# Routed gate and up projections with the weights stationary and the tokens streaming, each tile's weights brought from DRAM into a ring of six

## What is computed

```python
logits = jnp.einsum('th,eh->te', xt.astype(jnp.float32), w_router.astype(jnp.float32))
scores = jax.nn.sigmoid(logits)
topk_w, topk_i = jax.lax.top_k(scores, TOPK)
topk_w = topk_w / jnp.sum(topk_w, axis=-1, keepdims=True)
...
gate = jax.nn.silu(jnp.einsum('th,eih->tei', xt, wg))
up = jnp.einsum('th,eih->tei', xt, wu)
expert_out = jnp.einsum('tei,ehi->teh', gate * up, wd)
out = jnp.einsum('te,teh->th', comb, expert_out)
sgate = jax.nn.silu(jnp.einsum('th,jih->tji', xt, sg))
sup = jnp.einsum('th,jih->tji', xt, su)
out = out + jnp.einsum('tji,jhi->th', sgate * sup, sd)
```

## Time and profile before

| | |
|---|---|
| median of 3 runs | 445.16 us (443.85 to 445.98) |
| the profiled execution: its time | 445.5 us |
| the profiled execution: its span | 443.7 us |
| TensorE matmul busy | 395.6 us, 89% |
| TensorE loads busy | 289.1 us, 65% |
| DVE, ACT, POOL busy | 257.2, 205.5, 90.5 us |
| DMA traffic | 42.48 MB; HBM read 24.81 MB, written 17.31 MB |

### The profile page before, as it was taken

The page is one execution under the profiler, slowest core; times in us unless marked ns, Lnnn a source line. Parts: engine busy times, 40 slices in busy tenths (PEclk is TensorE's granted clock), DMA queues, the critical chain, the costliest instruction groups (busy, mean ns, idle before and its releaser), DMA issues.

```text
span 443.7 us, 7225 instructions
## 1 busy us (share of the span) xinstructions
PE 395.6 (89%) x2295; PEld 289.1 (65%) x2296; DVE 257.2 (58%) x814; ACT 205.5 (46%) x519; POOL 90.5 (20%) x100
## 2 busy tenths in 40 slices
PE   3877787787988999997999999999999999999991
PEld 2445464555765878776888886666667676766660
DVE  3799999899887784785474424343333333433330
ACT  4597999999854668420120213232232323232320
POOL 6656140001000022121312000212121212121221
PEclk9998999999998999998999999999999999999997
DMA  6199999100000001000698300122212222221212
GB/s 172 27 353 343 339 354 429 60 1 1 1 1 1 2 7 67 1 24 27 242 429 347 88 2 24 26 36 38 36 38 39 35 46 33 39 36 24 24 12 24
DMA packets 22988, 42.48 MB, mean 96 GB/s; under 512 B 1968, under 2 KB 20976, under 8 KB 21680
## 3 DMA queue, kind: packets, MB, share of 16 engines
q1 hardware_dynamic: 17632, 35.76, 23.3%
q0 software_dynamic: 4080, 5.18, 7.4%
q10 hardware_dynamic: 1248, 1.18, 0.8%
HBM read 24.81 MB, written 17.31 MB: 95 GB/s over the span
## 4 chain that ended last, share of the span: by engine, by line
PE 59%; DVE 19%; ACT 14%; POOL 3%; issue 2%; DMA 2%; POOLq 0%; DVEq 0%
PE ps_z L749 13%; PE ps_o L775 11%; PE ps_gu L749 9%; ACT weights L843 6%; PE ps_pt L605 5%; PE ps_z L598 5%; DVE weights L1041 5%; PE ps_gu L598 4%; DVE weights L1036 3%; ACT weights L834 3%; ACT weights L849 3%; PE ps_pt L765 3%; PE ps_gu L605 2%; DVE hidden L1094 1%; DVE gate_silu L1091 1%
## 5 line engine op out<-in xcount | busy, mean ns | idle before, releaser
L439 POOL DMA_INDIRECT out<-y_sb,tile_in x23 | 35.9, 1559 | 166.1 <-DVE y_sb L1280 163.0
L843 ACT ACTIVATE weights<-weights 128x256 f32<-128x256 f32 x128 | 64.3, 536 | 0.1
L749 PE MATMUL ps_z<-weights,tile_t 128*128 x184 | 63.2, 486 | 0.0
L775 PE MATMUL ps_o<-weights,hidden 128*128 x230 | 53.5, 380 | 0.9 <-ACT hidden L950 0.9
L1091 DVE SCALAR_TENSOR_TENSOR gate_silu<-gate_tanh,ps_z 128x256 f32<-128x256 f32 x66 | 24.5, 371 | 49.5 <-ACT gate_tanh L935 36.2
L517 PE MATMUL ps_pt<-ident,weights 128*128 128x128 f32 x256 | 35.4, 284 | 15.6 <-ACT weights L849 15.2
L749 PEld LDWEIGHTS ps_z<-weights,tile_t 128*128 128x128 f32 x184 | 33.2, 190 | 23.2 <-issue 22.0
L775 PEld LDWEIGHTS ps_o<-weights,hidden 128*128 128x128 f32 x230 | 43.6, 190 | 7.0 <-issue 1.1
L935 ACT ACTIVATE gate_tanh<-ps_gu 128x256 f32<-128x256 f32 x23 | 8.8, 383 | 80.5 <-PE ps_gu L749 80.5
L517 PEld LDWEIGHTS ps_pt<-ident,weights 128*128 128x128 f32 x256 | 29.9, 147 | 22.6 <-issue 21.8
L1036 DVE SCALAR_TENSOR_TENSOR weights<-weights 128x1024 f32<-128x1024 f32 x32 | 39.0, 1219 | 9.1 <-ACT weights L834 5.6
(11 more groups left out here) (192 smaller groups left out, 618.4 us busy)
## 6 DMA issues: line engine op xcount, KB each, us to landing
weights<-w_experts SPq DMA_DIRECT2D x8, 1920.0 KB, 14.1
slots<-pad_row SPq DMA_DIRECT2D x9, 1188.0 KB, 13.5
weights<-w_experts SPq DMA_DIRECT2D x1, 3840.0 KB, 14.5
tile_in<-slots SPq DMA_DIRECT2D x23, 132.0 KB, 2.1
out<-y_sb ACTq DMA_DIRECT2D x4, 256.0 KB, 2.2
weights<-x SPq DMA_DIRECT2D x2, 256.0 KB, 4.4
x_in<-x SPq DMA_DIRECT2D x2, 256.0 KB, 5.3
out<-y_sb,tile_in POOLq DMA_INDIRECT x23, 3.8
```

The source lines that it names most:

```text
L439: pool.indirect_dma_start(out=out, out_offset=bass.IndirectOffsetOnAxis(ap=tile_in[:, slot, ID_COL:ID_COL + 1].bitcast(U32), axis=0), in_= ...
L749: mm = pe.matmul(ps_chunk[c][:, 0:2 * cw], tile_t[:, r % 2, k, :], weights[:, bass.ds(off + (k * GU + 2 * c0), 2 * cw)], start=(k == 0), s ...
L775: mm = pe.matmul(ps_o[:, 0:D], hid_t[:, r % 2, i, :], weights[:, bass.ds(off + (KC * GU + i * D), D)], start=(i == 0), stop=(i == IC - 1))
L843: ins = act.activation(v, v, ACT.Exp, bias=neg_max[:, w % AHEAD, i:i + 1], scale=-1.0, accum_out=sums[:, L % PAIR, s:s + 1])
```

## The change

- The routed gate and up projections now have a 128x128 block of weights as stationary operand and stream the tile's 128 tokens (`gate_chunk`): 20 matmuls of 128 columns a tile in place of 4 of 512 and 2 of 256. Hidden columns come out on the partitions, and DVE writes them straight to `hid_t`.
- `turn_hidden` on TensorE, ACT's copy of its result (L950), and the semaphores between them are gone.
- In a TensorE step the down projection of tile j-1 moves ahead of chunks 1 and 2 of tile j. DVE scales tile j-1 in step j behind its first hidden chunk, one tile late where it was two.
- SBUF no longer holds the routed gate and up weights. The down weights of all eight experts (5.24 MB) are loaded in one DMA early on, behind the fill of `slots`. The gate and up weights of each tile's expert (1.31 MB: 128 partitions, 2 rows of 5,120 bytes each) are loaded for each of the 23 tiles into a ring of six places, which the attention's scratch shares; SP issues them behind the tile's rows, the first six once the table is ready, then one each time an add has landed. TensorE reads the ring at fixed addresses and waits for its semaphore at a tile's first chunk.
- The host lays the weights out in three arrays instead of one.

```diff
-        LATE = 5
-        scratch_at = [(E - LATE) * W_EXP]
+        scratch_at = [RING_AT]
...
-            for e in range(E - LATE):
-                sp.dma_start(w_exp[:, e, :], w_experts[e]).then_inc(ld_expert[e], 16)
+            sp.dma_start(weights[:, DOWN_AT:RING_AT].rearrange("p (e w) -> p e w", e=E),
+                         w_down.rearrange("e p w -> p e w")).then_inc(ld_down, 16)
+
+            def load_weights(j, place):
+                e = sp.value_load(expert_i[0:1, bass.ds(j, 1)], min_val=0, max_val=E - 1)
+                sp.dma_start(ring[place].rearrange("p (k w) -> p k w", k=KC),
+                             w_gu[bass.ds(e * (KC * P), KC * P), :].rearrange("(k p) w -> p k w", p=P)).then_inc(ld_ring[place], 16)
 
             sp.wait_ge(x_norm_ready, HV * B)
             sp.wait_ge(y_saved, PAIR)
             sp.wait_ge(st_early_rows, 16 * TOPK * HV * PAIR)
-            for e in range(E - LATE, E):
-                sp.dma_start(w_exp[:, e, :], w_experts[e]).then_inc(ld_expert[e], 16)
-
             sp.wait_ge(st_late_rows, 16 * TOPK * HV * (B - PAIR))
             sp.wait_ge(table_ready, 1)
             for j in range(SLOTS_IN):
                 load_tile(j, j)
+                load_weights(j, j)
...
                     sp.wait_ge(r_add, 16 * (j - SLOTS_IN + 1))
                     load_tile(j, s)
+                    load_weights(j, s)
...
-            def gate_chunk(q, r, c, off):
+            def gate_chunk(q, r, c):
                 j = SLOTS_IN * q + r
                 c0, cw = GATE_CHUNKS[c]
                 if c == 0:
+                    pe.wait_ge(ld_ring[r % SLOTS_IN], 16 * (q + r // SLOTS_IN + 1))
                     pe.wait_ge(r_xtc, j + 1)
                 if not isinstance(j, int) or j >= 1:
                     pe.wait_ge(r_hid, 3 * j + c - 2)
-                for k in range(KC):
-                    mm = pe.matmul(ps_chunk[c][:, 0:2 * cw], tile_t[:, r % 2, k, :],
-                                   weights[:, bass.ds(off + (k * GU + 2 * c0), 2 * cw)],
-                                   start=(k == 0), stop=(k == KC - 1))
+                for i in range(cw // P):
+                    for part, col in enumerate(gate_col(c0 // P + i)):
+                        for k in range(KC):
+                            a = k * GU + col
+                            mm = pe.matmul(ps_chunk[c][:, part * cw + i * P:part * cw + (i + 1) * P], ring[r % SLOTS_IN][:, a:a + P],
+                                           tile_t[:, r % 2, k, :], start=(k == 0), stop=(k == KC - 1))
                 mm.then_inc(r_gu, 1)
...
-            def turn_hidden(q, r):
...
-                pe.wait_ge(r_htc, j + 1)
+                pe.wait_ge(r_hid, 3 * j + 3)
...
             def step(q, r):
...
                 if inner or s >= 1:
-                    turn_hidden(q, r - 1)
-                if off is not None:
-                    gate_chunk(q, r, 1, off)
-                    gate_chunk(q, r, 2, off)
-                if inner or s >= 1:
                     down_tile(q, r - 1)
+                if inner or s < SLOT_TILES:
+                    gate_chunk(q, r, 1)
+                    gate_chunk(q, r, 2)
...
-                if inner or s >= 1:
-                    act.wait_ge(r_ht, s)
-                    act.activation(hid_t[:, (r - 1) % 2, :, :].rearrange("p a b -> p (a b)"), ps_pt[:, 0:I], ACT.Copy
-                                   ).then_inc(r_htc, 1)
...
-                if inner or s >= 2:
-                    scale_output(q, r - 2)
                 if inner or s < SLOT_TILES:
                     hidden_chunk(q, r, 0)
+                if inner or s >= 1:
+                    scale_output(q, r - 1)
+                if inner or s < SLOT_TILES:
                     hidden_chunk(q, r, 1)
                     hidden_chunk(q, r, 2)
```

More of the change, by code:

```diff
@@ L129, in build @@
         weights = sb("weights", [P, (E + NSH) * W_EXP])
+        ring = [weights[:, RING_AT + i * W_GU:RING_AT + (i + 1) * W_GU] for i in range(SLOTS_IN)]
         late_rows = [[sb(f"rows{n}{k}", [P, HV, ROW]) for k in range(TOPK)] for n in range(PAIR, B)]
@@ L219, in build @@
         ld_shared = sem("ld_shared")
-        ld_expert = [sem(f"ld_expert{e}") for e in range(E)]
+        ld_down = sem("ld_down")
+        ld_ring = [sem(f"ld_ring{i}") for i in range(SLOTS_IN)]
         const_step, ident_ready = sem("const_step"), sem("ident_ready")
@@ L747, in gate_chunk, with down_at @@
                     pe.wait_ge(r_hid, 3 * j + c - 2)
-                for k in range(KC):
-                    mm = pe.matmul(ps_chunk[c][:, 0:2 * cw], tile_t[:, r % 2, k, :],
-                                   weights[:, bass.ds(off + (k * GU + 2 * c0), 2 * cw)],
-                                   start=(k == 0), stop=(k == KC - 1))
+                for i in range(cw // P):
[4 more added lines that the diff above has]
+                                           tile_t[:, r % 2, k, :], start=(k == 0), stop=(k == KC - 1))
                 mm.then_inc(r_gu, 1)
-            def expert_at(q, r):
+            def down_at(q, r):
                 e = pe.value_load(expert_i[0:1, bass.ds(SLOTS_IN * q + r, 1)], min_val=0, max_val=E - 1)
-                return e * W_EXP
-            def turn_hidden(q, r):
[L760 to L764, removed]
-                    mm = pe.transpose(ps_pt[:, i * P:(i + 1) * P], hid[:, r % 2, i * P:(i + 1) * P], ident)
-                mm.then_inc(r_ht, 1)
+                return e * W_DOWN
             def down_tile(q, r):
                 j = SLOTS_IN * q + r
-                off = expert_at(q, r)
-                pe.wait_ge(r_htc, j + 1)
+                off = down_at(q, r)
+                pe.wait_ge(r_hid, 3 * j + 3)
                 if not isinstance(j, int) or j >= 1:
@@ L774, in down_tile @@
                 for i in range(IC):
-                    mm = pe.matmul(ps_o[:, 0:D], hid_t[:, r % 2, i, :],
-                                   weights[:, bass.ds(off + (KC * GU + i * D), D)], start=(i == 0), stop=(i == IC - 1))
+                    mm = pe.matmul(ps_o[:, 0:D], hid_t[:, r % 2, i * P:(i + 1) * P],
+                                   weights[:, bass.ds(off + (DOWN_AT + i * D), D)], start=(i == 0), stop=(i == IC - 1))
                 mm.then_inc(r_y, 1)
@@ L781, in step @@
                 inner = not isinstance(s, int)
-                off = expert_at(q, r) if inner or s < SLOT_TILES else None
-                if off is not None:
-                    gate_chunk(q, r, 0, off)
+                if inner or s < SLOT_TILES:
+                    gate_chunk(q, r, 0)
                 if inner or s + 1 < SLOT_TILES:
@@ L800, in _ @@
             shared_down(3, 1, 1)
-            for e in range(E):
-                pe.wait_ge(ld_expert[e], 16)
+            pe.wait_ge(ld_down, 16)
             step(0, 0)
@@ L1285, in step @@
                 inner = not isinstance(s, int)
-                if inner or s >= 2:
-                    scale_output(q, r - 2)
                 if inner or s < SLOT_TILES:
                     hidden_chunk(q, r, 0)
+                if inner or s >= 1:
+                    scale_output(q, r - 1)
+                if inner or s < SLOT_TILES:
                     hidden_chunk(q, r, 1)
                     hidden_chunk(q, r, 2)
-            for s in range(2):
-                step(0, s)
+            step(0, 0)
             dve.wait_ge(st_base, 16 * B)
-            for s in range(2, PEELED):
+            for s in range(1, PEELED):
                 step(0, s)
@@ L1300, in _ @@
                     step(q, r)
-            for s in range(PEELED + SLOTS_IN * ROUTED_LOOPS, SLOT_TILES + 2):
+            for s in range(PEELED + SLOTS_IN * ROUTED_LOOPS, SLOT_TILES + 1):
                 step(0, s)
@@ L1311, with gate_up_rows @@
     from concourse.bass_utils import run_bass_kernel_spmd
-    def expert_rows(gate, up, down):
+    def gate_up_rows(gate, up):
         n = gate.shape[0]
@@ L1321, in expert_rows, with down_rows, all_rows @@
             cols += [g[..., c0:c0 + cw], u[..., c0:c0 + cw]]
-        gu = np.concatenate(cols, -1).transpose(0, 2, 1, 3).reshape(n, P, KC * GU)
-        d = np.asarray(down).transpose(0, 2, 1).reshape(n, IC, P, D).transpose(0, 2, 1, 3).reshape(n, P, IC * D)
-        return np.concatenate([gu, d], -1)
+        return np.concatenate(cols, -1)
+    def down_rows(down):
+        n = down.shape[0]
+        return np.asarray(down).transpose(0, 2, 1).reshape(n, IC, P, D).transpose(0, 2, 1, 3).reshape(n, P, W_DOWN)
+    def all_rows(gate, up, down):
+        n = gate.shape[0]
+        return np.concatenate([gate_up_rows(gate, up).transpose(0, 2, 1, 3).reshape(n, P, W_GU), down_rows(down)], -1)
     arrays = {
```

36 lines of the change are left out of this document (20 added, 16 removed).

## The result

The changed kernel takes 443.03 us (median of 20 runs, 441.23 to 445.12), the kernel before beside it 445.58 us: ratio 0.9943, 95% interval 0.9926 to 0.9960. It is faster by 0.6%, where 1.9% was forecast and where the range ended at 442.5. The execution profiled took 441.58 us, one of the quicker ones; the predicted numbers are compared with it step by step.

A forecast was written before the change was run, and what follows sets the result against it. TensorE's own instructions were taken to bound the routed part. Steps -7.8, first step +0.2 and tail -1.1 gave -8.7 us from the profiled 445.5, or 436.8; less 0.3 to the median, 436.6 us, range 432.8 to 442.5.

The forecast's parts named there:

- the price of a pair: Routed gate and up: each weight load and 128-column matmul overlap at 0.112 us, making 4.48 us a tile.
- The step of 6.86: TensorE's routed step per tile falls from 7.21 to 6.86 us, saving 7.8 us over 22 steps.
- the first step of 4.70: The first routed step, with no hidden transposes before, grows by 0.18 us, from 4.52 to 4.70.
- the slack of the down projection: Before the moved down projection: hidden ready 1.3 us into the step, cover 2.0 us, slack 0.7, cost nothing.
- the first six ring loads: Weight loads before the routed part: 7.9 MB done by 259 us, first needed at 267, cost nothing.
- PEld near 330 us: Sign in the changed profile: PEld's busy time rises from 289 to near 330 us.
- The tail: After TensorE's last chunk: last add 5.0 us after the end instead of 6.17, giving -1.1 us.
- Weights, SP's queue: SP's weight loads: one of 1.31 MB, 3.3 us, per step of 6.86 us, SP having time to spare; cost nothing.
- the rival on POOL's adds: Routed loop: weight loads run into POOL's adds, 7.1 to 7.4 us an add, 7 us back, 443; chance 0.06.
- adds under 5 us: Sign in the changed profile: POOL's adds in the routed loop still take under 5 us.
- no idle time before the down projection: Sign in the changed profile: TensorE never idles before the routed down projection's matmuls.
- Its bad end: Worst form of the rival on POOL's adds: 8.8 us an add against 6.86, 17 times, +33 us, 470.

The follow-up runs named there:

- early_weights_5: The changed kernel with each weight load issued once TensorE finished gate and up of the tile six before, in more rounds: 436.45 us, 0.9811 of the kernel before.
- experiment 8: The kernel before with only the weight ring added, each load issued after the second chunk of tile m-5, between two adds: 446.04 us, 1.0016.
- experiment 2: The changed kernel with each weight load issued once TensorE finished gate and up of tile m-6, not at that tile's add landing: 437.66 us, 0.9795.
- experiment 5: The changed kernel with three places for scaled outputs instead of two: 444.78 us, 0.9972 of the kernel before.
- after_again: The changed kernel itself, unaltered, measured again in more rounds: 444.42 us, 0.9967 of the kernel before.
- experiment 11: The changed kernel with weight loads some 3.5 us later: 437.24 us, 0.9805; or issued before the tile's rows, 1.15 us sooner: 440.11 us, 0.9865.

## Why the prediction was wrong

**Right.** What bounded before, and the price of a pair (0.112 us), on which everything else hung: the 16 pairs of chunk 0 take 1.79. The rule of the Trainium skill (TensorE: Matmul & The Clock Gate, Back-to-back issue gap), by whose figures such pairs would take 45% longer than matmuls alone, does not hold for these float32 pairs: 920 of them run at the pace of the loads alone, with the clock at 1.00. The step of 6.86 (6.84; the gain over 22 steps is 7.7 us, where the prediction rounds to 7.8), the first step of 4.70 (265.45 to 270.13, 4.68), the gone transposes, the slack of the down projection (no wait until the adds ran late), the first six ring loads (no wait), and PEld near 330 us (329.0) came out. The tail too, where adds are on time: in early_weights_5 the last chunk ends at 422.54 and the last add is issued at 427.54, 5.0 us behind, as worked out. The sum, 436.6, is the time of a kernel with the same instructions and no collisions (436.45 to 437.66).

**Wrong: the step "Weights, SP's queue", where the load per step was costed at nothing,** and with it the weight given to the rival on POOL's adds (0.06). The load was priced by its bytes against SP's time and the ring's, and not by the add that it meets. The rival named the mechanism; these parts of it were off. Of the signs named beforehand, adds under 5 us (they took 6.7) and no idle time before the down projection (6.2 us) failed.

- Its period. I set an add's 3.8 us and the load's 3.3 us, 7.1 to 7.4, against the step. An add came to 6.6 to 7.9, but the chain also has 0.87 us from a landing to the next issue, which I had read from the earlier trace rows as the hop to POOL and not counted here. Issue to issue it is 7.5 to 8.8.
- The load's length. 3.3 us is 1.31 MB at the rate of five loads in flight; a single one takes 5.7 us in experiment 8, where it disturbs no add.
- Its phase. "When adds trail, POOL's 1.6 us of issuing falls before the weights flow" assumed that the add would be out of the way. SP starts from the same landing: it issues the rows and then the weights, most often 1.15 us behind the add's start, and POOL's instruction for the add, 1.56 us, is still running at that time. Being late locks add and load together, and keeps them late.
- Taking turns. The sentence on the queues (the Trainium skill, DMA: Bandwidth & Descriptors, SWDGE vs HWDGE vs iDMA) I read as letting the add through. The runs neither show nor exclude turns, but an add is not let through: loads with rows of 5,120 bytes hold it up by 2.9 us, of 1,280 by 1.8, of 10,240 by 3.6.

**Luck.** The rival's price, 0.4 x 17 = 7 us and 443, is the measured time, but not by its sum. Against the early reload of experiment 2, the 16 periods from 289.46 to 414.02 lose 15 us (124.6 against 109.6), twice what it had, and the last four periods win 8 back (18.3 against 26.4), because POOL works off its backlog at 4.6 us an add once no load is left. The rival had no such end. Its bad end, 8.8 us an add, rests on the 8.5 us of other transfers and 0.3 that no row gives.

The profiled run's sum with the measured terms, against the profiled execution of before: steps (7.11 - 7.21) x 22 = -2.2 in place of -7.8; first step +0.2; tail 5.7 (426.62 to 432.33) in place of 6.17, -0.5; what follows the last add 7.5 instead of 7.3, +0.2. That is -2.3. The steps and the tail are no causes of their own here, since the chain of adds sets both (experiment 5). Its routed part also began 1.6 us sooner (265.45 instead of 267.02), for which the change offers no clear reason; it varies from execution to execution: the same kernel has that start at 269.39 in after_again, and early_weights_5 at 267.52. Together 3.9 us, the difference of the spans.

## What to carry to other kernels

A transfer that is small against its step is not free when another engine's serial chain runs through the same DMA engines: price it by what it meets and when, with the chain's full period from issue to issue, and ask whether lateness moves the two together or apart. If a serial indirect add (or any short transfer that is waited for) shares the engines with bulk loads, time the loads so that they go out well behind the start of one add and well before the next (here 1.6 to 3.9 us behind its start), look at what stands ahead of them in the issuing queue, and keep their rows short. The pace of loads with almost nothing streaming, read from a router or any matmul of few columns, gave the price of load-bound matmul pairs to 1%.

## What the runs showed of the hardware

- Float32 loads of 128x128 and matmuls of 128 columns overlap fully, at 0.112 us a pair in runs of 16 and 24, at the clock's higher level, 2.4 GHz.
- An indirect add that meets a bulk load lands within about 1 us of it, in 6.6 to 7.9 us instead of 3.8 in the changed kernel. Issued 0.55 to 1.2 us ahead of the load it was always caught there, 1.55 us and more ahead (experiment 11) never; at 1.34 us both happened.
- Bulk rows of 1,280 bytes cost an add beside them half of what rows of 10,240 do (1.8 and 3.6 us), while the load itself takes longer (medians of all loads 7.5 and 6.1 us; few landings of the former are in the profile).
- Streaming 1.31 MB a step into SBUF (170 GB/s over the stage, DMA share 0.59) slowed no compute engine in experiment 8: TensorE stayed at 163.20 of 163.20 us, DVE at 60.5 (60.8 before) and ACT at 45.5.
